# Two constants of the norms in the first attention's loop: added by ScalarE as the bias of an Identity activation, instead of by VectorE

## The reference, cut to what matters

```python
x = x + L0_attn(layernorm(x, eps=1e-5))      # layernorm: (x - mean) / sqrt(var + eps)
x = x + L0_xattn(layernorm(x, eps=1e-5), ctx)
...
def L0_attn(x):                              # 16 heads of 8 channels
    attn = softmax(q @ k.T * 128 ** -0.5) + bias
    out = attn @ v
    return (out - mean(out)) / sqrt(var(out) + 1e-3) * gamma + beta
```

## Time and profile before

| | |
|---|---|
| median of 3 runs | 1639.27 us |
| the runs | 1628.08, 1642.25, 1639.27 us |
| profiled execution | 1629.23 us, span 1627.4 us |
| busy share of the span | TensorE 91%, VectorE 66%, ScalarE 53%, GpSimd 46% |
| the loop, 45 to 110 us | VectorE busy 59.43 us, TensorE 52.01, GpSimd 47.83, ScalarE 29.17 |

### The profile page before, as it was taken

One profiled execution on the slowest core, in us unless ns is written; L12 is line 12 of the kernel. 1 busy time (PEld: TensorE's weight loads), 2 busy tenths in 40 slices (PEclk: granted clock), 3 DMA queues, 4 the chain that ended last, 5 costly groups with the idle time before them and its releaser, 6 DMA issues.

```text
span 1627.4 us, 41073 instructions
## 1 busy us (share of the span) xinstructions
PE 1475.6 (91%) x17022; PEld 947.9 (58%) x17022; DVE 1066.2 (66%) x1723; ACT 868.7 (53%) x1783; POOL 744.2 (46%) x670
## 2 busy tenths in 40 slices
PE   7879999999999799857699999999999999889998
PEld 4557888765444466525466666666666666555554
DVE  6885555433342377686588888888888888634554
ACT  3432333345654233315577777777777777743333
POOL 6773111100000057767488777778777776000000
PEclk9879999989999799968899999999999999989999
DMA  4003000041210420245555555464654654403320
GB/s 120 2 1 107 2 2 2 2 128 45 78 39 13 86 60 23 45 98 103 128 129 130 120 125 130 121 132 118 135 127 124 125 130 110 111 1 93 68 57 14
DMA packets 62539, 129.54 MB, mean 80 GB/s; under 512 B 15793, under 2 KB 38066, under 8 KB 59186
## 3 DMA queue, kind: packets, MB, share of 16 engines
q1 hardware_dynamic: 62354, 126.92, 33.5%
HBM read 100.22 MB, written 26.67 MB: 78 GB/s over the span
## 4 chain that ended last, share of the span: by engine, by line
PE 33%; POOL 11%; ACT 8%; issue 2%; DVE 2%; DMA 1%; SPq 0%; ACTq 0%; POOLq 0%; DVEq 0%
PE ps L1724 7%; POOL ARENA L1928 7%; PE ps L865 7%; PE ps L1708 5%; POOL ARENA L1934 4%; PE ps L877 3%; PE ps L1671 3%; ACT ARENA L1878 3%; PE ps L1662 2%; ACT ARENA L1856 2%; PE ps L1685 2%; ACT ARENA L1869 1%; ACT ARENA L1862 1%; PE ps L1733 1%; DVE ARENA L1798 1%
## 5 line engine op out<-in xcount | busy, mean ns | idle before, releaser
L1798 DVE TENSOR_REDUCE ARENA<-ps 112x2 f32<-112x1000 f32 x384 | 456.7, 1198 | 118.0 <-PE ps L1685 115.1
L1878 ACT ACTIVATE ARENA<-ps 125x448 f32<-125x448 f32 x768 | 378.4, 549 | 127.9 <-PE ps L1708 127.0
L1928 POOL TENSOR_TENSOR ARENA<-ARENA 64x500 f32<-64x500 f32 x192 | 264.8, 1379 | 104.4 <-ACT ARENA L1856 85.9
L107 POOL TENSOR_TENSOR rs<-rs,mhalf 128x1 f32<-128x1 f32 x96 | 57.7, 602 | 363.5 <-DVE rs L102 363.2
L865 PE MATMUL ps<-XT,ARENA 128*128 128x448 f32 x544 | 219.9, 549 | 0.0
L1708 PEld LDWEIGHTS ps<-ARENA 64*125 64x125 bf16 x3072 | 122.5, 134 | 133.3 <-ACT ARENA L1878 70.3
L1708 PE MATMUL ps<-ARENA 64*125 64x112 bf16 x3072 | 168.9, 228 | 20.0 <-ACT ARENA L1878 18.8
L1724 PE MATMUL ps<-ARENA 125*17 125x112 f32 x6144 | 184.9, 260 | 0.0
L865 PEld LDWEIGHTS ps<-XT,ARENA 128*128 128x128 f32 x544 | 104.6, 194 | 99.1 <-issue 98.7
L877 PE MATMUL ps<-ARENA 128*128 128x448 f32 x400 | 161.6, 539 | 0.0
L1685 PE MATMUL ps<-ARENA 64*112 64x500 bf16 x768 | 152.7, 387 | 9.0 <-DVE ARENA L1798 8.9
(11 more groups left out here) (228 smaller groups left out, 2106.2 us busy)
## 6 DMA issues: line engine op xcount, KB each, us to landing
ARENA<-key_parts SPq DMA_DIRECT2D x192, 187.5 KB, 4.1
ARENA<-in_ctxT SPq DMA_DIRECT2D x96, 250.0 KB, 3.8
key_parts<-ARENA SPq DMA_DIRECT2D x64, 375.0 KB, 2.7
ARENA<-token_weights SPq DMA_DIRECT2D x32, 512.0 KB, 5.6
ARENA<-in_L_ffn_W SPq DMA_DIRECT2D x1, 2048.0 KB, 8.8
ARENA<-query_parts SPq DMA_DIRECT2D x6, 192.0 KB, 6.0
ARENA<-in_c_ones SPq DMA_DIRECT2D x2, 562.5 KB, 14.7
ARENA<-in_L_attn_a SPq DMA_DIRECT2D x2, 512.0 KB, 5.3
```

Source lines behind the costliest of these rows:

```text
L1798: e.tensor_reduce(mxp[0:112, b % 2, 2 * g:2 * g + 2, ch], ps[0:112, b1:b1 + 2, 0:500], AX, ALU.max) \
L1878: e.activation(Pb[0:KT, n % NP_, 448 * h:448 * h + 448], ps[0:KT, b1[h], 0:448], ACT.Exp, bias=0.0, scale=1.0).then_inc(exped.sem, 1)
L1928: e.tensor_tensor(T2[r:r + 64, :], T0[64 - r:128 - r, n % 2, :], sin[64 - r:128 - r, sl], ALU.mult) \
```

## The change

In iteration t ScalarE now adds both constants, as the bias of an activation with function Identity, read from a new tile `eps` of two columns. The first stands behind its two copies L418, the second behind the exponential L422. VectorE no longer has L365 and L102 in this loop (L102 stays in all other places). GpSimd fills `eps` at the start with two memsets.

```diff
+        eps = sb("eps", [128, 2])
...
+        def ln_floor(e, w, k, t):
+
+            n = 16 * k + t
+            w.wait_ge(*eps_set(2))
+            w.wait_ge(*ln_var(n + 1))
+            e.activation(rs[:, t:t + 1], mv[:, t, 1:2], ACT.Identity, bias=eps[:, 0:1], scale=1.0).then_inc(ln_eps.sem, 1)
...
             e.memset(mhalf[:, :], -0.5).then_inc(half_set.sem, 1)
+            for i, v in enumerate((1e-5, 1e-3)):
+                e.memset(eps[:, i:i + 1], v).then_inc(eps_set.sem, 1)
...
                         e.bn_aggr(mv[:, v, :], st[:, v, :]).then_inc(post_var.sem, 1)
-                        w.wait_ge(*post_var(v + 1))
-                        e.tensor_scalar(rs[:, v:v + 1], mv[:, v, 1:2], 1e-3, None, ALU.add).then_inc(post_eps.sem, 1)
...
                         w.wait_ge(*added(t - 3))
-                        ln_stats(e, w, 1, t - 4)
+                        ln_moments(e, w, 1, t - 4)
...
+                    v = t - 3
+                    if 0 <= v < NT:
+                        w.wait_ge(*eps_set(2))
+                        w.wait_ge(*post_var(v + 1))
+                        e.activation(rs[:, v:v + 1], mv[:, v, 1:2], ACT.Identity, bias=eps[:, 1:2], scale=1.0) \
+                            .then_inc(post_eps.sem, 1)
                     if t < NT:
                         w.wait_ge(*shifted(t + 1))
                         e.activation(E[:, t % 3], E[:, t % 3], ACT.Exp, bias=0.0, scale=1.0).then_inc(exped.sem, 1)
+                    if 4 <= t < NT + 4:
+                        ln_floor(e, w, 1, t - 4)
                     if t >= 5:
                         ln_copy(e, w, 1, t - 5, at["ln", t - 5])
```

More of the change, by code:

```diff
@@ L92, in decoder, with ln_moments @@
         ln_inv, ln_x, ln_t, ln_out = (signal("ln_" + n, 96) for n in ("inv", "x", "t", "out"))
-        xr_zero, half_set = signal("xr_zero", 4), signal("half_set", 1)
+        xr_zero, half_set, eps_set = signal("xr_zero", 4), signal("half_set", 1), signal("eps_set", 2)
         x_in, id_in = [signal("x_in%d" % n, 2, 16) for n in range(4)], signal("id_in", 1, 16)
-        def ln_stats(e, w, k, t):
+        def ln_moments(e, w, k, t):
             n = 16 * k + t
@@ L100, in ln_stats @@
             e.bn_aggr(mv[:, t, :], st[:, t, :]).then_inc(ln_var.sem, 1)
+        def ln_stats(e, w, k, t):
+            n = 16 * k + t
+            ln_moments(e, w, k, t)
             w.wait_ge(*ln_var(n + 1))
             e.tensor_scalar(rs[:, t:t + 1], mv[:, t, 1:2], 1e-5, None, ALU.add).then_inc(ln_eps.sem, 1)
+        def ln_floor(e, w, k, t):
+            n = 16 * k + t
+            w.wait_ge(*eps_set(2))
+            w.wait_ge(*ln_var(n + 1))
+            e.activation(rs[:, t:t + 1], mv[:, t, 1:2], ACT.Identity, bias=eps[:, 0:1], scale=1.0).then_inc(ln_eps.sem, 1)
         def ln_power(e, w, k, t):
```

## The result

With the change the kernel takes 1639.70 us (median of 22 runs, 1634.71 to 1647.38), beside 1630.54 us for 22 runs of the kernel before. The ratio is 1.0042, 95% interval 1.0026 to 1.0058: 0.4% slower, some 7 us by the ratio (the two medians are 9.2 us apart). The whole interval lies on the slower side, and well within the 1% (16 us) that the prediction took as what can be told from no change. The profiled execution has a span of 1638.4 us (1627.4 before).

The account below looks back on a forecast made before the run. VectorE was taken to bound the loop, TensorE just behind at low clock. Loop +1.5, loop's end +0.8 and stage boundary +1.2 gave +3.5 us, added to the earlier runs' mean 1636.5: 1640.0 us, range 1628 to 1650.

Parts of the forecast that it names:

- The price of an addition: VectorE's loop: each removed addition frees 0.19 us, 0.38 an iteration, at most 6.1 us over all 32.
- The activations: ScalarE: each of the 32 new 128x1 activations that add a constant takes 0.30 us.
- Rival C: ScalarE's loop: Identity and Exp share no function table, so three loads an iteration; about 1655 us, chance 0.03.
- The first floor's wait: First constant's addition, behind ScalarE's copies: at low clock its power comes late and VectorE stands 1.07 us at L387.
- The circle through Exp, second floor and GpSimd: Second constant's addition behind Exp delays GpSimd's queue and then VectorE: two iterations take 9.86 us, 4.93 each.
- The boundary: Start of next stage: tile 15's second constant waits behind that stage's front on ScalarE, first scores 1.2 us later.
- The loop's end: Iteration 16: GpSimd's L107 waits for both additions behind ScalarE's second copy, +0.8 us.
- The loop: Twelve full iterations of the first attention: +1.5 us, taken between -2.2 and +3.7.
- every second one at low clock: Twelve full loop iterations, alternate ones with TensorE's clock low: 6 x 0.62 = +3.7 us, the upper end.
- rival B: Loop: low clock in nearly all iterations, 5.99 us each, +12.5 us with the ends, 1649 us; chance 0.14.
- operation beside GpSimd: VectorE's loop before: it holds the rest of the 0.37 us by which a low-clock iteration exceeds 4.93.

Follow-up runs that it names:

- the transposes: The change plus 8 identity transposes on TensorE before its wait for the normalised tile, iterations 5 to 15; ratio 0.9977 to the kernel before.
- the floor back on VectorE: The change, but from iteration 16 on (for the first constant, tile 13) VectorE adds both constants again; ratio 1.0025 to the kernel before.
- no constants: The kernel before with both constants of this loop left out, GpSimd taking the power of the bare variance; ratio 0.9958.
- the shifted floors: The change with both additions ahead of ScalarE's copies, the second an iteration later, and VectorE adding both from iteration 16; ratio 0.9967 to the kernel before.
- the first floor alone: The change with only the first constant (1e-3, behind the copies) on ScalarE and the second back on VectorE; ratio 1.0057 to the kernel before.

## Why the prediction was right

The time, 1639.70 us, is nearly the 1640.0 forecast, and a difference below 1% had 0.93 of the chance. That the two times are so close is luck: two errors cancelled. The waits that it named are all there, but not every term of the sum had its size.

- *The price of an addition*, 0.19 us: 4.93 us went to 4.72 with one gone, 4.51 with both, so 0.21 each. Right.
- *The activations*: 0.30 us and 0.29 us. Right. Rival C: the groups of the kernel with the change show the same loads as before, none of them at a line of the loop but the one at the very start (L141 is the L129 of before):

```profile
L927 ACT ACT_TABLE_LOAD x3 | 3.8, 1283 | 0.1
...
L141 ACT ACT_TABLE_LOAD x1 | 1.3, 1283 | 0.7 <-PEq L2196 0.7
```

- *The first floor's wait*: at a low clock 98.78 - 97.81 = 0.97 us were forecast from its start to L387; 69.67 - 68.71 = 0.96 measured. Right. The longest waits are 1.5 us, longer than the 1.07 forecast.
- *The circle through Exp, second floor and GpSimd*: 9.86 us for two iterations were forecast, 5.17 + 4.61 = 9.78 measured, with the clock held up by the transposes. The forecast had two equal iterations of 4.93; they alternate.
- *The boundary*: +1.2 forecast, 2.33 - 1.25 = +1.08 measured, and gone with the floor back on VectorE.
- *The loop's end*: +0.8 forecast. From the second copy to L114 it was 116.80 - 110.88 = 5.92; now it is 122.66 - 115.60 = 7.06, +1.14. The step left out the first power, which stands ahead of L107 on GpSimd and now waits for ScalarE as well:

```profile
115.60 0.58 ACT L430 COPY ARENA<-ps 112x512 f32<-112x512 f32 x1 [0.21 <-PE ps L316]
...
116.46 0.55 POOL L481 TENSOR_TENSOR rs<-rs,mhalf 128x1 f32<-128x1 f32 x1 [0.81 <-ACT rs L436]
116.97 0.55 POOL L119 TENSOR_TENSOR rs<-rs,mhalf 128x1 f32<-128x1 f32 x1
...
122.66 0.34 DVE L126 TENSOR_SCALAR xn<-XR,mv,rs 128x128 f32<-128x128 f32 x1
```

- *The loop*: +1.5 us forecast for twelve iterations, +5.55 measured in ten of them, above the +3.7 of its upper end. This is the term that was mis-sized. The step that failed is "every second one at low clock" as the upper end: five iterations in a row took 5.62 to 6.26 us, which is what rival B had for each (5.99). B, at 0.14, came partly true: not in all iterations, since two of 4.59 us stood among them.

The sum was therefore too small: +3.5 us against +7.72 to the first scores in the profile, and 9.2 between the medians. The forecast of 1640.0 came out right because the kernel before was set at the mean of its three runs, 1636.5, and its median over 22 runs is 1630.54, 6.0 lower. A ratio of 1.002 was forecast; 1.0042 was measured.

What stays open is why the clock was low more often with the change. Longer waits of TensorE alone do not explain it: it was 0.50 from 58 to 70 us with waits of 0.4 us, and it was also 0.76 with no constants and 0.73 with the shifted floors, where VectorE has no wait for a floor. The runs show what the low clock costs and that work in the wait lifts it, not what brings it on in each of these kernels.

The scatter is open too. The change's 22 runs order by their mean clock: 1634.71 us at 0.955, 1647.38 us at 0.942. That goes with a loss by the clock, but where in the program each run lost it is not in a time. The 3.3 us behind the stage in the profiled execution, and that the ratio fell by more than the first scores moved in the kernel with the change and the transposes, belong to that. Why the first floor alone costs about as much as both was not taken apart further than by the clocks.

## What to carry to other kernels

An instruction of 0.15 us moved to an idle engine costs what stands ahead of it in that engine's order: place it by when its input is ready and its output needed, not in the order of the code. Where TensorE waits in every iteration and its clock swings, look at the clock in windows of an iteration beside the waits: the first floor alone made no wait at the upper clock, and cost 9.8 us in ten iterations at 0.67. Try idle work in TensorE's wait; with the change eight transposes of the identity were worth 0.65%, while in the kernel before no gain in time is shown (0.9959 to 1.0006).

## What the runs showed of the hardware

Work in the wait moves the clock. In the kernel before TensorE stood 2.02 us for the normalised tile and was at 0.52 in the 3 us behind it. With eight transposes of 128x128 in that wait the clock stayed at 1.00 for ten iterations, though TensorE still waited 0.61 us in most of them.

VectorE's sum of two SBUF tiles, usually 0.29 us, took 1.51 us in the kernel without constants, while GpSimd built the head masks from 63.21 to 64.90:

```profile
63.21 1.69 POOL L447 TENSOR_TENSOR ARENA<-ARENA 128x896 f32<-128x896 f32 x1
...
63.53 1.51 DVE L372 TENSOR_TENSOR ARENA<-ARENA 128x128 f32<-128x128 f32 x1
```

It ended 0.14 us behind GpSimd's instruction, as if it had waited for it within its own duration. The Trainium skill, SBUF — State Buffer ("SBUF: two separate sides"), says that on the engines' side only the pair of ports shared by VectorE and GpSimd causes contention, and that an instruction of VectorE with two SBUF inputs and one of GpSimd that reads SBUF exclude each other: the later one waits for the whole of the other. These rows agree. Meeting GpSimd's long instruction thus cost VectorE 1.2 us, with no wait to be seen in the list of waits. The kernel with the shifted floors shows it too, once, at 1.24 us, in its iteration of 6.80 us. In the kernel before the same sum (L358) lasted 0.49 to 0.51 us in the four iterations of 5.3 us: these 0.2 us are the prediction's "operation beside GpSimd".
